# A fourth pair of weight chunks joins the split products of samples 4 to 6

## The chip, the cores and the metric

The kernel runs on 1 core of one Trainium2 chip. The metric is the device time of one execution in microseconds (us); lower is better.

## The reference, cut to what matters

There are eight samples of 256 tokens, each with 1024 features. For each sample a weight matrix (1024x1024) is picked by an index and applied; a quantised feed-forward block follows and is added to the input. A second block (a shared matrix with a low-rank addition, then a mixing of four streams with 50 Sinkhorn rounds) follows.

```
x = x + ffn0(einsum('bij,bkj->bik', x, weight[ids]))     # ffn0: layernorm, int8-quantised w1, gelu, quantised w3
y = x @ base.T + bias + scale * low_rank(x)
x = x + stream_mixing(y)                                 # softmaxes, Sinkhorn, W_branch
```

Only the first product, `x` by `weight[ids]`, is touched by the change. Its result is kept in float32 precision.

## The kernel before, in words

There is no scheduler: each engine's program is written out by hand, and engines meet only at semaphores. A wait holds back everything behind it on its engine. The first block is worked in steps `s` (`step_a`, one on each engine). In step `s` TensorE makes the indexed product of sample `s`, and between its parts the quantised products of samples `s-1` (w1) and `s-2` (w3). The 1024 inputs of the indexed product are worked in four pairs of 128-row chunks (`pr` 0 to 3), and `l0(s, pr)` on TensorE is one such pair, for two token tiles and two halves of 512 outputs.

A pair is worked in one of two ways. Plain (line 1010): 8 matmuls on float32 operands, which the profile shows as 16 records. Parted (line 998): ScalarE copies the pair's `x` and `w` rounded to float32r as high parts (`pair_high`, lines 726 to 732), VectorE subtracts them from the raw values in place to get low parts (`pair_low`, lines 1543 to 1547), and TensorE makes high x high, high x low and low x high: 24 matmuls. Before the change samples 3 to 6 take pairs 0, 1 and 2 parted and pair 3 plain; samples 0 to 2 and 7 are plain throughout.

The orders around it, as written by hand:

- TensorE in step `s` (lines 1140 to 1166): transposes and w3 product of `s-2` between `l0(s,0)` and `l0(s,1)`; transposes of `s-1`, tile 0; `l0(s,2)`; w1 product of `s-1`, tile 0; transposes of tile 1; `l0(s,3)`; w1 product of `s-1`, tile 1. Step 4 ends with `composites_1` (line 1121), which multiplies eight 512 KB chunks of the base weight, loaded into `stage[0]` to `stage[7]`, by the head weights. The first matmul of `l0(s,0)` waits until ScalarE has emptied the accumulators of sample `s-1` (`evac_l0`, line 633).
- ScalarE in step `s` (lines 756 to 806): first quantisation of `s-1` tile 0; `pair_high(s,2)`; evacuations (line 672); `pair_high(s+1,0)` and `(s+1,1)`; quantisation of tile 1 (line 652); evacuation; gelu (line 657) and second quantisation (line 661) of `s-1` tile 0; `evac_l0(s)`; and so on. In steps 6 and 7 it also makes the high parts of the base weight (`split_hi`, line 616): `split_hi(1)` stands behind the second quantisation of sample 5 tile 0, `split_hi(2)` ahead of gelu, root and second quantisation of sample 5 tile 1.
- VectorE in step `s` (lines 1549 to 1573): normalisation of `s-1` tile 0; `finish_w3(s-2,0)`; `pair_low(s,2)`; `layer_norm(s-1,1)`; `finish_w3(s-2,1)`; `pair_low(s+1,0)`, `(s+1,1)`; `finish_w1(s-1,0)` (lines 1461, 1465, 1471 to 1476); `scale_w1(s-1,1)` and so on.
- GpSimd makes the low parts of the base weight (`split_lo`, line 571), each when its high part is there, and adds a bias row to the residual (line 577).
- SyncE issues nearly all DMAs in one order. `load_w(s,pr)` is 1 MB of weights and 256 KB of `x`, and for sample 7 waits until GpSimd has made `split_lo(pr)`. In step 6 its order ends with `load_w(7,1)`, `load_base(3)`, `store_head_rows`, `load_w(7,2)`, `load_w(7,3)`. `store_head_rows` (lines 356 to 359) writes two small arrays, `heads_in` and `bias_in`, to DRAM and counts on `all_st`, which reaches 64 when both have landed.

Buffers overlap by hand as well. `w_hi[3]` lies on `stage[6]` and `stage[7]`, and on `heads_in` and `bias_in`; `w_hi[2]` lies on `stage[4]` and `stage[5]`. Hence this wait, ahead of the last high part:

```
                if pr == PAIRS - 1:
                    act.wait_ge(all_st, 64)
                nc.scalar.activation(w_hi[pr][:, :, :], w_raw[pr][:, :, :], ACT.Copy).then_inc(whi_done, 1)
```

Of the kernel before, what the change touches and what calls it, by code (L numbers as in the profile page):

```python
# [25 lines left out]
def adaln_ffn(nc, x_tok, x_tr, cond_w, ids_cond, ids_lora, gamma, beta, w1, b1, w3, b3, base_w, base_w_nat,  # L26
# [15 lines left out]
    HG = GROUP // 2  # L42
    MIX = 4
    GUEST = NB - 1
    FIRST = 3
    HEADS_1, HEADS_2, HEADS_3 = 4, 5, 6
    TQ = P // NS
    SEL_BANK = 4
# [16 lines left out]
    with ExitStack() as ctx:  # L65
# [14 lines left out]
        one_hi = sb_in(part_e, "one_hi", [1, D], F32R)  # L80
        part_e.close()
        part_n = ctx.enter_context(ExitStack())
        for i in range(2 * PAIRS - 2):
            sb_in(part_n, f"below_heads{i}", [P, D], F32)
        heads_in = sb_in(part_n, "heads_in", [NB * RANK, NH], F32)
        heads_hi = sb_in(part_n, "heads_hi", [NB * RANK, NH], F32R)
# [26 lines left out]

        def parted(s, pr):

            return FIRST <= s < GUEST and pr < PAIRS - 1

        def w_high(pr):

            return w_lo[pr]  # L120

        def x_high(s, pr):

# [1 line left out]

        def parts(s, pr):

            return 2 * (s - FIRST + 1)

        def pair_loads(s, pr):  # L130

# [99 lines left out]


        vec_ld, bias_ld, ids_ld, ones_set = sem("vec_ld"), sem("bias_ld"), sem("ids_ld"), sem("ones_set")
        high = [sem(f"high{i}") for i in range(PAIRS - 1)]
        low = [sem(f"low{i}") for i in range(PAIRS - 1)]
        id_zero, id_set, id16_set = sem("id_zero"), sem("id_set"), sem("id16_set")
        misc_ld, wb_split, b_set, b_ld = sem("misc_ld"), sem("wb_split"), sem("b_set"), sem("b_ld")
        st_ld = [sem(f"st_ld{i}") for i in range(ST)]
# [5 lines left out]
        wld = [sem(f"wld{i}") for i in range(PAIRS)]  # L244
        first_ld = sem("first_ld")
        whi_done, wlo_done, l0_pair, l0_evac = sem("whi_done"), sem("wlo_done"), sem("l0_pair"), sem("l0_evac")
        ln_mean, ln_var = sem("ln_mean"), sem("ln_var")
        ln_step, ln_sqrt, q1_done, q2_done = sem("ln_step"), sem("ln_sqrt"), sem("q1_done"), sem("q2_done")
        t1_done, e1_done, m1_done, o1_done = sem("t1_done"), sem("e1_done"), sem("m1_done"), sem("o1_done")
        t3_done, e3_done, m3_done, o3_done = sem("t3_done"), sem("e3_done"), sem("m3_done"), sem("o3_done")  # L250
# [47 lines left out]
        def _(sp):  # L298
# [100 lines left out]
            load_w(2, 3)  # L399

            def step_a(s):
                nat = KC if s == HEADS_1 else 0
                load_w(s + 1, 0)
                for c in range(0, nat, 2):
                    load_nat(c)
                load_w(s + 1, 1)
                store_x1(s - 2, 0)
                for c in range(1, nat, 2):
                    load_nat(c)
                load_w(s + 1, 2)  # L410
                store_x1(s - 2, 1)
                load_w(s + 1, 3)
                load_xres(s - 1)

            def step_a_base(s):
                load_base(0)
                store_x1(s - 2, 0)
                load_base(1)
                load_w(s + 1, 0)
                store_x1(s - 2, 1)  # L420
                load_base(2)
                load_xres(s - 1)
                load_w(s + 1, 1)
                load_base(3)
                store_head_rows()
                load_w(s + 1, 2)
                load_w(s + 1, 3)

# [181 lines left out]
        def _(act):  # L610
            def split_hi(pr):

                act.wait_ge(wld[pr], pair_loads(GUEST - 1, pr) + 16)
                if pr == PAIRS - 1:
                    act.wait_ge(all_st, 64)
                nc.scalar.activation(w_hi[pr][:, :, :], w_raw[pr][:, :, :], ACT.Copy).then_inc(whi_done, 1)

# [18 lines left out]
            def statistics(s, t):  # L636
                j = NTOK * s + t
                act.wait_ge(l0_evac, j + 1)
                nc.scalar.activation(lnst[:, t, 0:1], lnst[:, t, 1:2], ACT.Copy, scale=-1.0 / D).then_inc(ln_mean, 1)
                act.wait_ge(ln_mean, j + 1)  # L640
                wait(act, x1_st[t], 16 * (s - 1))
                nc.scalar.activation(ln_sq(s, t)[:, :], hbuf[t][:, :], ACT.Square, bias=lnst[:, t, 0:1],
                                     accum_out=lnst[:, t, 10:11]).then_inc(ln_var, 1)

            def ln_root(s, t):
                j = NTOK * s + t
# [79 lines left out]
            def pair_high(s, pr):  # L726
                if s < NB and parted(s, pr):
                    act.wait_ge(wld[pr], pair_loads(s, pr))
                    if s == FIRST:
                        act.wait_ge(all_st, 32)  # L730
                    nc.scalar.activation(x_high(s, pr), x_raw[pr][:, :, :], ACT.Copy).then_inc(high[pr], 1)
                    nc.scalar.activation(w_high(pr)[:, :, :], w_raw[pr][:, :, :], ACT.Copy).then_inc(high[pr], 1)
# [23 lines left out]
            def step_a(s):  # L756
                quant1(s - 1, 0)
                if s == 2:
                    rows_high()
                pair_high(s, 2)  # L760
                if s == HEADS_2:
                    composites_2()
                evac_T(s - 2, 1, 3)
                if s == GUEST:
                    split_hi(3)
                ln_root(s - 1, 1)
                evac_T(s - 1, 0, 1)
                pair_high(s + 1, 0)
# [36 lines left out]
                quant2(s - 1, 1)  # L805
                statistics(s, 1)
# [583 lines left out]
        def _(dve):  # L1390
# [26 lines left out]
            def centre(s, t):  # L1417

                h = hbuf[t]
                dve.wait_ge(ln_var, NTOK * s + t + 1)  # L1420
# [128 lines left out]
            def step_a(s):  # L1549
                normalise(s - 1, 0)  # L1550
                if s == 2:
                    rows_low()
                    dve.wait_ge(sc_ev, 2)
                if s == FIRST:
                    gate_first()
                if s == HEADS_2:
                    composites()
# [1 line left out]
                pair_low(s, 2)  # L1559
                layer_norm(s - 1, 1)  # L1560
                finish_w3(s - 2, 1)
                pair_low(s + 1, 0)
                pair_low(s + 1, 1)
                finish_w1(s - 1, 0)
# [342 lines left out]
```

## Time and profile before

| what | us |
|---|---|
| median of 3 runs (749.0 to 750.52) | 749.83 |
| the profiled execution, its own time | 751.13 |
| span of the profiled execution, first to last instruction | 749.3 |
| TensorE busy in it | 707.8 (94%) |
| VectorE busy | 526.2 (70%) |
| ScalarE busy | 397.3 (53%) |
| GpSimd busy | 79.9 (11%) |

The profile is of one execution. All times in rows are microseconds from the start of its span. The granted clock of TensorE had a mean of 0.977 of full speed. Steps 4, 5 and 6 of the first block fill the stretch from 166 to 305 us. A busy TensorE isn't TensorE at its peak, because matmuls overlap and their ends are modelled; the chain of work is the better measure of what one block of matmuls costs.

### The profile page before, as it was taken

The numbers are of one execution on the slowest core, as the hardware profiler recorded it, in microseconds if no ns is written. First come the engines' busy times: TensorE is split into PE (matmuls) and PEld (weight loads), VectorE is DVE, ScalarE is ACT, GpSimd is POOL, SyncE is SP. The second block draws the span as 40 slices with busy tenths as digits, with TensorE's granted clock in tenths as the row PEclk, the third lists the DMA queues.
The fourth block names the chain that finished last, engine by engine and source line by source line (L and its number), as shares of the span: only waits on it lengthen the run. The fifth ranks groups of instructions, "written<-read, shape, count | busy, mean of one in ns | idle before, by whom it ended". The sixth has DMA issues, their size and how long they took to land.

```text
span 749.3 us, 10394 instructions
## 1 busy us (share of the span) xinstructions
PE 707.8 (94%) x3292; PEld 477.6 (64%) x3292; DVE 526.2 (70%) x1869; ACT 397.3 (53%) x714; POOL 79.9 (11%) x57
## 2 busy tenths in 40 slices
PE   8999999999999999999998999999999993999957
PEld 5444445656536565445656888887888872677656
DVE  4569676979742976776663341428899998999985
ACT  1255846666741584828355443444534432899614
POOL 0201400302030032732040000000000000000000
PEclk9999999999999999999998999999999996999979
DMA  7997255558734236851232303303123086847106
GB/s 297 409 410 284 94 196 207 187 165 300 294 111 169 101 126 197 327 199 64 69 127 74 127 13 115 127 0 128 56 74 128 0 281 224 262 162 244 64 1 224
DMA packets 52477, 124.35 MB, mean 166 GB/s; under 512 B 6211, under 2 KB 31939, under 8 KB 46920
## 3 DMA queue, kind: packets, MB, share of 16 engines
q1 hardware_dynamic: 51128, 120.96, 45.6%
q10 hardware_dynamic: 1296, 2.74, 1.0%
q8 instruction: 26, 0.43, 0.2%
q14 instruction: 27, 0.22, 0.1%
HBM read 97.96 MB, written 25.72 MB: 165 GB/s over the span
## 4 chain that ended last, share of the span: by engine, by line
PE 74%; DVE 19%; ACT 5%; issue 2%; DMA 1%; SPq 0%; ACTq 0%; DVEq 0%
PE PS L1204 20%; PE PS L1010 18%; PE PS L1087 13%; PE PS L998 8%; DVE kprod L1725 4%; DVE ksum L1729 4%; PE PS L1192 2%; PE PS L1019 2%; DVE ka L1732 2%; DVE kb L1732 2%; PE PS L1356 2%; PE PS L1121 2%; PE PS L1178 2%; PE PS L1238 1%; PE PS L1366 1%
## 5 line engine op out<-in xcount | busy, mean ns | idle before, releaser
L1010 PE MATMUL PS<-w_raw,x_raw 128*128 128x512 f32 x320 | 141.7, 596 | 1.3 <-DMA w_raw<-cond_w_dram 0.9
L1010 PEld LDWEIGHTS PS<-w_raw,x_raw 128*128 128x128 f32 x320 | 59.4, 190 | 69.6 <-issue 69.6
L1204 PE MATMUL PS<-w_hi,xT_hi 128*128 128x512 f32 x256 | 103.0, 402 | 0.0
L1204 PE MATMUL PS<-w_hi,xT_lo 128*128 128x512 f32 x256 | 100.5, 393 | 0.0
L1204 PE MATMUL PS<-w_lo,xT_hi 128*128 128x512 f32 x256 | 100.4, 392 | 0.0
L1539 DVE TENSOR_TENSOR xT_lo<-PS,xT_hi 128x512 fp32r<-128x512 f32 x32 | 20.5, 682 | 66.0 <-ACT xT_hi L753 66.0
L1729 DVE TENSOR_REDUCE ksum<-kprod 128x16 f32<-128x64 f32 x392 | 66.3, 211 | 0.0
L577 POOL TENSOR_TENSOR xres<-xres,vecs 128x1024 f32<-128x1024 f32 x16 | 42.5, 2680 | 218.1 <-DMA xres<-x_tok_dram 218.1
L672 ACT ACTIVATE qT<-PS,round_c 128x1024 bf16<-128x1024 f16 x32 | 35.4, 1108 | 56.6 <-PE PS L1019 56.6
L1087 PE MATMUL PS<-w3q,qT 128*128 128x512 bf16 x256 | 57.8, 379 | 1.0 <-ACT qT L672 1.0
L1087 PE MATMUL PS<-w1q,qT 128*128 128x512 bf16 x256 | 57.9, 379 | 0.3 <-ACT qT L672 0.3
L1204 PEld LDWEIGHTS PS<-w_hi,xT_lo 128*128 128x128 f32 x256 | 48.3, 189 | 10.4
L1204 PEld LDWEIGHTS PS<-w_lo,xT_hi 128*128 128x128 f32 x256 | 48.5, 190 | 9.2
L1204 PEld LDWEIGHTS PS<-w_hi,xT_hi 128*128 128x128 f32 x256 | 48.6, 190 | 9.1
L833 ACT ACTIVATE y<-PS 128x512 f32<-128x512 f32 x32 | 18.0, 592 | 57.0 <-PE PS L1212 57.0
L1087 PEld LDWEIGHTS PS<-w1q,qT 128*128 128x128 bf16 x256 | 24.5, 98 | 32.6 <-issue 5.5
L1087 PEld LDWEIGHTS PS<-w3q,qT 128*128 128x128 bf16 x256 | 24.2, 98 | 33.2 <-issue 4.4
L1461 DVE SCALAR_TENSOR_TENSOR gbuf<-PS,lnst,vecs 128x512 f32<-128x512 f32 x32 | 23.5, 748 | 30.9 <-PE PS L1087 30.8
L998 PE MATMUL PS<-w_lo 128*128 128x512 f32 x96 | 38.6, 402 | 1.2 <-DVE w_low L1547 1.0
L998 PE MATMUL PS<-w_lo,x_low 128*128 128x512 f32 x96 | 38.0, 395 | 0.0
L998 PE MATMUL PS<-w_low,w_lo 128*128 128x512 f32 x96 | 37.8, 394 | 0.0
L1488 DVE SCALAR_TENSOR_TENSOR x1buf<-PS,q2st,vecs 128x512 f32<-128x512 f32 x32 | 23.0, 746 | 19.1 <-PE PS L1087 19.1
(209 smaller groups left out, 1358.0 us busy)
## 6 DMA issues: line engine op xcount, KB each, us to landing
w_raw<-cond_w_dram SPq DMA_DIRECT2D x31, 1024.0 KB, 5.4
x_raw<-x_tr_dram SPq DMA_DIRECT2D x32, 256.0 KB, 6.7
stage<-w_dram SPq DMA_DIRECT2D x16, 512.0 KB, 16.2
xres<-x_tok_dram SPq DMA_DIRECT2D x8, 1024.0 KB, 8.2
x_scratch<-x1buf SPq DMA_DIRECT2D x16, 512.0 KB, 6.7
x1n<-x_scratch SPq DMA_DIRECT2D x16, 512.0 KB, 6.6
y_scratch<-y SPq DMA_DIRECT2D x16, 512.0 KB, 3.7
stage<-base_w_nat_dram SPq DMA_DIRECT2D x8, 512.0 KB, 8.7
```

Source lines behind the costliest of these rows:

```text
L577: nc.gpsimd.tensor_tensor(xres[:, t, :], xres[:, t, :], vecs[:, V_B3, :], ALU.add).then_inc(xb3_done, 1)
L672: nc.scalar.activation(qT[t][:, :, :], PS[:, T_BANK + t, :].bitcast(F16).rearrange("p (c n) -> p c n", c=KC), ACT.Identity, bias=round_c[: ...
L998: mm = pe.matmul(PS[:, 2 * t + h, :], xx[:, c, t * P:(t + 1) * P], ws[:, c, h * H2:(h + 1) * H2], start=(pr == 0 and c == 0 and xx is xh a ...
L1010: mm = pe.matmul(PS[:, 2 * t + h, :], x_raw[pr][:, c, t * P:(t + 1) * P], w_raw[pr][:, c, h * H2:(h + 1) * H2], start=(pr == 0 and c == 0) ...
L1087: mm = pe.matmul(PS[:, O_BANK + h, :], qT[t][:, c, :], wq[:, c, h * H2:(h + 1) * H2], start=(c == 0), stop=(c == KC - 1))
L1204: pe.matmul(PS[:, 2 * t + h, :], xx[:, c, t * P:(t + 1) * P], ws[c // 2][:, c % 2, h * H2:(h + 1) * H2], start=(c == 0 and xx is xT_hi and ...
L1461: nc.vector.scalar_tensor_tensor(out=g[:, h * H2:(h + 1) * H2], in0=PS[:, O_BANK + h, :], scalar=lnst[:, t, 8:9], in1=vecs[:, V_SW1, h * H ...
L1488: nc.vector.scalar_tensor_tensor(out=x1buf[t][:, h * H2:(h + 1) * H2], in0=PS[:, O_BANK + h, :], scalar=q2st[:, t, 1:2], in1=vecs[:, V_SW3 ...
L1539: nc.vector.tensor_tensor(xT_lo[:, 4 * h:4 * h + 4, t * P:(t + 1) * P], PS[:, T_BANK + h, :].rearrange("p (c n) -> p c n", c=4), xT_hi[:, ...
L1725: nc.vector.tensor_tensor(kprod[i][:, :, :, :], (kmat if row else kmat_t)[i][:, :, :, :], cols(v, HG), ALU.mult).then_inc(k_step[i], 1)
L1729: nc.vector.tensor_reduce(ksum[i][:, :, :], kprod[i][:, :, :, :], AX.X, ALU.add).then_inc(k_step[i], 1)
L1732: nc.vector.reciprocal(new[i][:, :, :], ksum[i][:, :, :]).then_inc(k_step[i], 1)
```

## The change

Pair 3 of samples 4, 5 and 6 becomes parted. Its high `w` goes into `w_hi[3]`, its high `x` into the last quarter of `w_lo[3]`. `pair_high(s,3)` is put on ScalarE behind the evacuation of tile 0, `pair_low(s,3)` on VectorE behind `finish_w3(s-2,1)`, in both cases ahead of the parts of the next sample. Since `w_hi[3]` is now in use during step 4, chunks 6 and 7 of the base weight are loaded at the end of that step, behind `load_w(5,3)`. Since it is in use until step 6, `heads_in` and `bias_in` move down by two buffers, onto `w_hi[2]`; so `split_hi(2)` and no longer `split_hi(3)` waits for `all_st`, and `store_head_rows` is issued ahead of `load_base(3)`. Two semaphores of the statistics become one with doubled counts.

```
-    FIRST = 3
+    FIRST = (3, 3, 3, 4)
...
-        for i in range(2 * PAIRS - 2):
+        for i in range(2 * PAIRS - 4):
             sb_in(part_n, f"below_heads{i}", [P, D], F32)
...
-            return FIRST <= s < GUEST and pr < PAIRS - 1
+            return FIRST[pr] <= s < GUEST
...
-            return w_lo[pr]
+            return w_hi[pr] if pr == PAIRS - 1 else w_lo[pr]
...
-            return 2 * (s - FIRST + 1)
+            return 2 * (s - FIRST[pr] + 1)
...
-        high = [sem(f"high{i}") for i in range(PAIRS - 1)]
-        low = [sem(f"low{i}") for i in range(PAIRS - 1)]
+        high = [sem(f"high{i}") for i in range(PAIRS)]
+        low = [sem(f"low{i}") for i in range(PAIRS)]
...
-        ln_mean, ln_var = sem("ln_mean"), sem("ln_var")
+        ln_stat = sem("ln_stat")
...
             def step_a(s):
-                nat = KC if s == HEADS_1 else 0
+                nat = KC - 2 if s == HEADS_1 else 0
...
                 load_w(s + 1, 3)
+                for c in range(nat, KC if nat else 0):
+                    load_nat(c)
                 load_xres(s - 1)
...
                 load_w(s + 1, 1)
+                store_head_rows()
                 load_base(3)
-                store_head_rows()
...
-                if pr == PAIRS - 1:
+                if pr == PAIRS - 2:
                     act.wait_ge(all_st, 64)
...
                     split_hi(3)
                 ln_root(s - 1, 1)
                 evac_T(s - 1, 0, 1)
+                if s < GUEST:
+                    pair_high(s, 3)
                 pair_high(s + 1, 0)
                 pair_high(s + 1, 1)
                 quant1(s - 1, 1)
...
                 layer_norm(s - 1, 1)
                 finish_w3(s - 2, 1)
+                if s < GUEST:
+                    pair_low(s, 3)
                 pair_low(s + 1, 0)
                 pair_low(s + 1, 1)
                 finish_w1(s - 1, 0)
```

## Rows read from the trace of the kernel before

**Rows 1.** The page: TensorE's busy time, and GB/s moved in 40 slices.

```profile
PE 707.8 (94%) x3292; PEld 477.6 (64%) x3292; DVE 526.2 (70%) x1869; ACT 397.3 (53%) x714; POOL 79.9 (11%) x57
...
GB/s 297 409 410 284 94 196 207 187 165 300 294 111 169 101 126 197 327 199 64 69 127 74 127 13 115 127 0 128 56 74 128 0 281 224 262 162 244 64 1 224
```

**Rows 2.** The chain that ended last, step 4: start, duration, what.

```profile
186.00 5.62 PE PS L998 x24
...
195.53 6.92 PE PS L1010 x16
...
205.91 0.89 issue
206.80 13.89 PE PS L1121 x32
```

**Rows 3.** Timeline of VectorE, step 4: start, duration, line, operation, tiles, idle time before.

```profile
193.39 0.68 DVE L1546 TENSOR_TENSOR x_low<-x_raw,w_lo 128x512 fp32r<-128x512 f32 x1
...
196.19 1.40 DVE L1461 SCALAR_TENSOR_TENSOR gbuf<-PS,lnst,vecs 128x512 f32<-128x512 f32 x2
...
205.95 0.75 DVE L1461 SCALAR_TENSOR_TENSOR gbuf<-PS,lnst,vecs 128x512 f32<-128x512 f32 x1 [0.91 <-PE PS L1087]
```

**Rows 4.** The DMA issues of the page: count, KB each, us to landing.

```profile
stage<-base_w_nat_dram SPq DMA_DIRECT2D x8, 512.0 KB, 8.7
```

**Rows 5.** The chain that ended last, end of step 5.

```profile
255.17 2.20 DVE w_low L1547
257.37 1.33 DVE gbuf L1461 x2
...
263.86 1.10 ACT hbuf L633 x2
...
265.10 5.82 PE PS L998 x24
```

**Rows 6.** Timeline of ScalarE, steps 4, 6 and 7.

```profile
187.11 0.62 ACT L731 ACTIVATE w_lo<-x_raw 128x512 fp32r<-128x512 f32 x1
...
189.44 0.61 ACT L731 ACTIVATE w_lo<-x_raw 128x512 fp32r<-128x512 f32 x1
...
299.12 1.24 ACT L661 ACTIVATE gbuf<-gbuf,round_c,q2st 128x1024 f32<-128x1024 f32 x1 [1.67 <-DVE q2st L1476]
...
307.17 1.90 ACT L616 ACTIVATE w_hi<-w_raw 128x2048 fp32r<-128x2048 f32 x1
...
311.69 1.24 ACT L661 ACTIVATE gbuf<-gbuf,round_c,q2st 128x1024 f32<-128x1024 f32 x1 [0.16 <-DVE q2st L1476]
```

**Rows 7.** Timeline of GpSimd, step 6.

```profile
290.14 4.52 POOL L571 TENSOR_TENSOR w_lo<-w_raw,w_hi 128x2048 fp32r<-128x2048 f32 x1 [14.12 <-ACT w_hi L616]
302.24 4.54 POOL L571 TENSOR_TENSOR w_lo<-w_raw,w_hi 128x2048 fp32r<-128x2048 f32 x1 [7.58 <-ACT w_hi L616]
```

**Rows 8.** Timeline of VectorE, step 6.

```profile
294.25 1.50 DVE L1465 TENSOR_TENSOR gbuf<-gbuf,vecs 128x1024 f32<-128x1024 f32 x1
...
305.07 2.78 DVE L1465 TENSOR_TENSOR gbuf<-gbuf,vecs 128x1024 f32<-128x1024 f32 x1
```

**Rows 9.** Timeline of SyncE's DMA queue, steps 5 to 7.

```profile
261.16 0.35 SPq L320 DMA_DIRECT2D w_raw<-cond_w_dram  x1
...
270.44 0.24 SPq L350 DMA_DIRECT2D bias_in<-biashead_scratch  x1
...
306.96 0.35 SPq L320 DMA_DIRECT2D w_raw<-cond_w_dram  x1
...
309.11 0.43 SPq L358 DMA_DIRECT2D stack_low_scratch<-heads_in  x1
```

**Rows 10.** Timeline of TensorE, step 7.

```profile
314.90 0.61 PE L1019 MATMUL PS<-ident,gbuf 128*128 128x128 f16 x8
```

**Rows 11.** Timeline of TensorE, later: a pause.

```profile
403.05 1.19 PE L1212 MATMUL PS<-es,ls 128*128 128x512 f32 x4 [1.56 <-DVE ls L1581]
```

**Rows 12.** Busy time by stretch: length, each engine's busy time (instructions), granted clock, DMA.

```profile
404.00:412.00 8.00, 6.90 (x31) 5.89 (x30) 2.76 (x6) 7.69 (x17) 0.46 (x1) 0.57 0.03 9
```

More of the change, by code:

```diff
@@ L44, in adaln_ffn @@
     GUEST = NB - 1
-    FIRST = 3
+    FIRST = (3, 3, 3, 4)
     HEADS_1, HEADS_2, HEADS_3 = 4, 5, 6
@@ L82, in adaln_ffn @@
         part_n = ctx.enter_context(ExitStack())
-        for i in range(2 * PAIRS - 2):
+        for i in range(2 * PAIRS - 4):
             sb_in(part_n, f"below_heads{i}", [P, D], F32)
@@ L114, in parted @@
         def parted(s, pr):
-            return FIRST <= s < GUEST and pr < PAIRS - 1
+            return FIRST[pr] <= s < GUEST
         def w_high(pr):
-            return w_lo[pr]
+            return w_hi[pr] if pr == PAIRS - 1 else w_lo[pr]
         def x_high(s, pr):
@@ L126, in parts @@
         def parts(s, pr):
-            return 2 * (s - FIRST + 1)
+            return 2 * (s - FIRST[pr] + 1)
         def pair_loads(s, pr):
@@ L233, in adaln_ffn @@
         vec_ld, bias_ld, ids_ld, ones_set = sem("vec_ld"), sem("bias_ld"), sem("ids_ld"), sem("ones_set")
-        high = [sem(f"high{i}") for i in range(PAIRS - 1)]
-        low = [sem(f"low{i}") for i in range(PAIRS - 1)]
+        high = [sem(f"high{i}") for i in range(PAIRS)]
+        low = [sem(f"low{i}") for i in range(PAIRS)]
         id_zero, id_set, id16_set = sem("id_zero"), sem("id_set"), sem("id16_set")
@@ L246, in adaln_ffn @@
         whi_done, wlo_done, l0_pair, l0_evac = sem("whi_done"), sem("wlo_done"), sem("l0_pair"), sem("l0_evac")
-        ln_mean, ln_var = sem("ln_mean"), sem("ln_var")
+        ln_stat = sem("ln_stat")
         ln_step, ln_sqrt, q1_done, q2_done = sem("ln_step"), sem("ln_sqrt"), sem("q1_done"), sem("q2_done")
@@ L401, in step_a @@
             def step_a(s):
-                nat = KC if s == HEADS_1 else 0
+                nat = KC - 2 if s == HEADS_1 else 0
                 load_w(s + 1, 0)
@@ L412, in step_a @@
                 load_w(s + 1, 3)
+                for c in range(nat, KC if nat else 0):
+                    load_nat(c)
                 load_xres(s - 1)
@@ L423, in step_a_base @@
                 load_w(s + 1, 1)
+                store_head_rows()
                 load_base(3)
-                store_head_rows()
                 load_w(s + 1, 2)
@@ L613, in split_hi @@
                 act.wait_ge(wld[pr], pair_loads(GUEST - 1, pr) + 16)
-                if pr == PAIRS - 1:
+                if pr == PAIRS - 2:
                     act.wait_ge(all_st, 64)
@@ L638, in statistics @@
                 act.wait_ge(l0_evac, j + 1)
-                nc.scalar.activation(lnst[:, t, 0:1], lnst[:, t, 1:2], ACT.Copy, scale=-1.0 / D).then_inc(ln_mean, 1)
-                act.wait_ge(ln_mean, j + 1)
+                nc.scalar.activation(lnst[:, t, 0:1], lnst[:, t, 1:2], ACT.Copy, scale=-1.0 / D).then_inc(ln_stat, 1)
+                act.wait_ge(ln_stat, 2 * j + 1)
                 wait(act, x1_st[t], 16 * (s - 1))
                 nc.scalar.activation(ln_sq(s, t)[:, :], hbuf[t][:, :], ACT.Square, bias=lnst[:, t, 0:1],
-                                     accum_out=lnst[:, t, 10:11]).then_inc(ln_var, 1)
+                                     accum_out=lnst[:, t, 10:11]).then_inc(ln_stat, 1)
             def ln_root(s, t):
@@ L728, in pair_high @@
                     act.wait_ge(wld[pr], pair_loads(s, pr))
-                    if s == FIRST:
+                    if s == FIRST[0]:
                         act.wait_ge(all_st, 32)
@@ L767, in step_a @@
                 evac_T(s - 1, 0, 1)
+                if s < GUEST:
+                    pair_high(s, 3)
                 pair_high(s + 1, 0)
@@ L1419, in centre @@
                 h = hbuf[t]
-                dve.wait_ge(ln_var, NTOK * s + t + 1)
+                dve.wait_ge(ln_stat, 2 * (NTOK * s + t + 1))
                 nc.vector.tensor_scalar(lnst[:, t, 2:3], lnst[:, t, 10:11], 1.0 / D, LN_EPS, ALU.mult, ALU.add).then_inc(ln_step, 1)
@@ L1553, in step_a @@
                     dve.wait_ge(sc_ev, 2)
-                if s == FIRST:
+                if s == FIRST[0]:
                     gate_first()
@@ L1561, in step_a @@
                 finish_w3(s - 2, 1)
+                if s < GUEST:
+                    pair_low(s, 3)
                 pair_low(s + 1, 0)
```

## The prediction

> **What bounds the kernel now.** I read the page first: TensorE is busy 94% of the span [rows 1], so a shorter product on TensorE should shorten the kernel, unless another engine is what ends the waits there. Then the chain that ended last, in order of time. In step 4 it is TensorE all the way, with 0.89 us of pause ahead of `composites_1` [rows 2]. A parted pair takes 5.62 us of it and the plain one 6.92 us: 1.30 us for each of three pairs, 3.9 us in all, is what the edit offers.
>
> At the end of step 5 the chain isn't TensorE's. It goes through VectorE's `w_low` for pair 1 of the next sample, then without a pause into `gbuf` (L1461, the start of `finish_w1(4,0)`), through gelu and second quantisation into the evacuation `evac_l0(5)` at 263.86, and only then into `l0(6,0)` at 265.10 [rows 5]. Whatever is put on VectorE ahead of `finish_w1` there is paid in full.
>
> **Step 4.** The low parts of a pair cost VectorE 2.80 us (start to start, 193.39 to 196.19) [rows 3], the high parts cost ScalarE 2.33 us (187.11 to 189.44) [rows 6]. `finish_w1(3,0)` moves from 196.19 to 199.0. Its way to the start of the second quantisation is 5.35 us, by the same way in step 5 (257.37 to 263.86, less 1.15 for the quantisation) [rows 5, 6], so VectorE is free at 204.4 and has the two halves of `scale_w1(3,1)` done 1.4 us later, at 205.8. `composites_1` waits for exactly that; before it came 0.1 us behind the second half, which ended at 206.70 [rows 2, 3]. So it starts at 205.9: the gain of step 4 is 0.9 and not 1.3 us. ScalarE's extra 2.33 us delays the quantisation of tile 1 by as much, to about 195.3, some 0.2 us behind where TensorE asks for it; this is inside the 0.4 lost.
>
> Chunks 6 and 7 are now issued behind `load_w(5,3)`, near 202.4. A chunk takes 8.7 us to land [rows 4]; chunk 6 is wanted at three quarters of the 13.89 us of `composites_1` [rows 2], at 216.3, chunk 7 at 218. I cost this at nothing; the residual load behind them gets later by the 2.6 us that 1 MB takes at 410 GB/s, the page's best early slice [rows 1], and nothing asks for it soon. If that cover were gone the price would be some us, ahead of step 5.
>
> **Step 5.** Everything starts 0.9 us early, VectorE then gets 2.80 us more ahead of `finish_w1(4,0)`: +1.9. `evac_l0(5)` ends and `l0(6,0)` starts at 267.0 and not at 265.1. TensorE has meanwhile saved its 1.3 us, and waits.
>
> **Step 6.** `l0(6,3)` saves 1.3 us on TensorE, but the other engines get busier. ScalarE has 2.33 us more ahead of `split_hi(0)`, so GpSimd can begin its first split some 2.8 us later than 290.14 [rows 7]. What that does is in two rows: `gbuf` (L1465) at 294.25 took 1.50 us and ended 1.09 us behind the end of GpSimd's split (290.14 + 4.52); at 305.07 it took 2.78 us and ended 1.07 us behind the next (302.24 + 4.54) [rows 7, 8]. That VectorE operation stands still until GpSimd is done. With GpSimd's split ending at 297.4 to 298.8, the add of `finish_w1(5,0)` ends at 298.5 to 299.9 instead of 295.75, and the second quantisation of sample 5 tile 0, at 299.12 before [rows 6], is later by 2.1 to 3.5 us. I take 3.0. Behind it on ScalarE stands `split_hi(1)`, behind that GpSimd's `split_lo(1)`, and for that SyncE waits before `load_w(7,1)`: from 306.96 [rows 9] to 310.0.
>
> **Step 7, the moved wait.** `split_hi(2)` ran at 307.17 with nothing to wait for [rows 6]. Now it waits for `all_st`, and the two stores that raise it are issued on SyncE only behind `load_w(7,1)`. Moving them ahead of `load_base(3)` helps little: before they were issued at 309.11, 2.15 us behind `load_w(7,1)` with `load_base(3)` between [rows 9]; now some 1.7 us behind it. All of them are queued behind 1.25 MB. The trace has no row for their landing, but a near one: two small stores behind `load_w(6,3)`, with 1 MB of residual between, were waited for until 270.44, 9.3 us after that load was issued at 261.16 [rows 9]. Less 2.6 us for the 1 MB leaves 6.7 us. Bounds: 1.9 us after the load is issued (they land at once) and 9.3 us. I take 6.7, the same queue with the same load ahead: `split_hi(2)` starts at 316.7 (bounds 311.9 and 319.3).
>
> The Trainium skill speaks against the change here (DMA: Bandwidth & Descriptors, section Queues, rings and completion order): an engine's count on the semaphore lands only after every earlier write of that DMA engine. By it the small stores count no sooner than the 1.25 MB ahead has landed, and the lower bound falls away; that agrees with the 9.3 us of the row.
>
> Queued behind `split_hi(2)` on ScalarE are gelu, root and second quantisation of sample 5 tile 1. That quantisation starts 4.52 us behind `split_hi(2)` (307.17 to 311.69) and takes 1.15 [rows 6]; TensorE's transposes of it, between `product(5,0,3)` and `l0(7,1)`, follow at 316.7 + 5.8 = 322.5. They ran at 315.0 [rows 10], when TensorE was just ready for them. **So TensorE's work restarts 7.5 us late** (bounds 317.7 and 325.1: +2.7 and +10.1), and nearly all of it is a pause: it would have been ready by 317. GpSimd's splits and the loads for pairs 2 and 3 of sample 7 follow `split_hi(2)` too, but TensorE has two pairs of 7 us each and two products before it asks for the last.
>
> **The clock.** A pause of 5 to 6 us hasn't been free in this trace. After one of 1.56 us at 403.05 and 1.1 us more [rows 11] the granted clock fell, and had a mean of 0.57 over the eight us from 404, that is, mostly at the lower level of 1.2 GHz [rows 12]. That cost at most 0.43 x 8 = 3.4 us, less where TensorE paused anyway. I take 2.5 (bounds 0 and 3.4).
>
> **The sum.** The step 4 and 5 terms (-0.9, +2.8), the step 6 term (+1.1 on the way through ScalarE and GpSimd) and the wait for the stores are all within the +7.5; +2.5 for the clock makes +10.0. From 410 us on the order of work is the same and TensorE-bound or Sinkhorn-bound, so nothing is won back. Against the profiled execution's 751.13 that gives 761.1; it lies 1.3 above the median of the runs, so in their terms 749.83 + 10.0 = **759.8 us**. The folded semaphore of the statistics adds and removes no instruction and no wait that ends later: nothing.
>
> **The rivals.**
> 1. The pause comes as told but is short, or the clock stays up: the stores land early or GpSimd doesn't get in VectorE's way. +2.7 to +7, 752.5 to 757. For it: no row times these stores. Against: the 9.3 us of the neighbour.
> 2. The stores are harmless, and only VectorE's queue in step 5 costs. Then `l0(7,0)` starts when `evac_l0(6)` is done: `split_hi(1)` ahead of it is 3.0 late, so some +1.5: 751.3. It decides if `all_st` is up by 310. Against: SyncE doesn't even issue the stores until then.
> 3. All is hidden and TensorE alone counts: 3 x 1.3 = -3.9, 745.9. It would need `finish_w1(4,0)` to have slack in step 5; the chain shows none [rows 5]. If the copies took less time on VectorE than the 2.80 of their twins, it would come nearer.
> 4. Both pauses (the one ahead of `l0(6,0)` is some 3 us in two pieces) drop the clock and the stores take the full 9.3: +10.1 + 3.4 = +13.5, 763.3, or somewhat more.
> That the parted pair 3 isn't faster than the plain one is hardly open: the shapes are those of pairs 0 to 2.
>
> **Chances.** Forecast with a drop in the clock, 757 to 763.3: 0.62. Rival 1: 0.20. Rival 2: 0.08. Rival 3: 0.04. Rival 4 and beyond: 0.06. About 0.2% (1.5 us) is what a measurement of this kernel can tell from no change. Faster by more 0.05, within 0.08, slower 0.87. The range, 753.0 to 763.5, holds the forecast and rival 1.
>
> **What would show it.** Right: L998 x24 at 5.6 us for pair 3; `composites_1` about 0.9 us earlier; `l0(6,0)` near 267; two small stores issued near 312; an idle time of ScalarE of 6 to 9 us ahead of the `split_hi` of pair 2, ended by a DMA; TensorE idle ahead of L1019 near 317, 4 to 7 us; a granted clock under 1 near 322 to 328. Wrong: `split_hi(2)` with no idle time before it, or `l0(6,0)` at 265 or earlier.

## The result and the profile after

| | median us (lowest to highest, runs) | against the kernel before, 95% interval |
|---|---|---|
| before | 750.17 (749.0 to 751.2, 4) | |
| after | 762.97 (761.02 to 764.68, 4) | 1.0173 [1.0154, 1.0193] |

The change makes the kernel 12.8 us slower. The forecast was 759.8 us with a range of 753.0 to 763.5: the sign and the place were right, the median lies 3.2 us above the forecast and inside the range. The profiled execution took 761.02 us (span 759.1); it is the fastest of the four, and stands 9.9 us above the profiled execution of before, where +10.0 was forecast.

The page's totals. TensorE is busy for less time than before [rows 1], in a span 9.8 us longer: the shorter product is there, and it doesn't decide.

```profile
PE 705.0 (93%) x3316; PEld 480.1 (63%) x3316; DVE 537.8 (71%) x1875; ACT 404.2 (53%) x720; POOL 80.1 (11%) x57
```

The chain that ended last, from step 4 to step 7 (start, duration, what):

```profile
195.48 5.61 PE PS L1002 x24
...
205.46 13.89 PE PS L1125 x32
...
256.62 2.21 DVE w_low L1551
258.83 1.33 DVE gbuf L1465 x2
...
266.56 7.35 PE PS L1002 x24
...
292.95 3.48 PE PS L1091 x16
...
297.24 2.65 DVE gbuf L1469
...
303.80 1.90 ACT w_hi L618
305.77 4.54 POOL w_lo L573
...
311.82 6.32 DMA stack_low_scratch<-bias_in
318.23 1.91 ACT w_hi L618
...
324.05 1.03 PE PS L1023 x8
325.08 8.87 PE PS L1014 x16
...
337.85 6.92 PE PS L1014 x16
```

Pair 3 now takes 5.61 us (first line) instead of 6.92 [rows 2]. `composites_1` starts at 205.46 instead of 206.80. From step 5 on the kernel is late: `l0(6,0)` starts at 266.56 instead of 265.10 [rows 5] and then takes 7.35 us instead of 5.82. Near 300 the chain has left TensorE altogether and runs through VectorE, ScalarE, GpSimd and two small stores to TensorE's restart at 324.05. Before, the same transposes started at 314.90 [rows 10]. In the order of time (us from the start of the span):

| event | before | after | forecast |
|---|---|---|---|
| `composites_1` starts | 206.80 | 205.46 | 205.9 |
| `l0(6,0)` starts | 265.10 | 266.56 | 267.0 |
| second quantisation, sample 5 tile 0 | 299.12 | 302.65 | 302.1 |
| `load_w(7,1)` issued | 306.96 | 310.48 | 310.0 |
| `split_hi(2)` starts | 307.17 | 318.23 | 316.7 |
| TensorE's transposes behind it start | 314.90 | 324.05 | 322.5 |

The end of the chain's detour, on SyncE's queue:

```profile
310.48 0.35 SPq L320 DMA_DIRECT2D w_raw<-cond_w_dram  x1
...
311.35 0.43 SPq L358 DMA_DIRECT2D stack_low_scratch<-heads_in  x1
311.82 0.42 SPq L359 DMA_DIRECT2D stack_low_scratch<-bias_in  x1
```

and on ScalarE:

```profile
302.65 1.24 ACT L663 ACTIVATE gbuf<-gbuf,round_c,q2st 128x1024 f32<-128x1024 f32 x1 [1.68 <-DVE q2st L1480]
...
318.23 1.91 ACT L618 ACTIVATE w_hi<-w_raw 128x2048 fp32r<-128x2048 f32 x1 [8.16 <-DMA stack_low_scratch<-bias_in]
```

Here ScalarE stood for 8.16 us at the moved wait, with gelu and the second quantisation of tile 1 queued behind it. The last of the small stores had landed 7.7 us after `load_w(7,1)` was issued.

TensorE's own timeline shows the two pauses:

```profile
265.47 0.62 PE L1023 MATMUL PS<-ident,gbuf 128*128 128x128 f16 x8 [2.22 <-ACT gbuf L663]
...
324.05 1.03 PE L1023 MATMUL PS<-ident,gbuf 128*128 128x128 f16 x8 [6.66 <-ACT gbuf L663]
```

and the windows by stretch (length, busy time of PE, PEld, DVE, ACT, POOL, granted clock, DMA share, GB/s) show what stands behind each:

```profile
268.00:272.00 4.00, 4.00 (x13) 3.12 (x12) 2.17 (x2) 3.95 (x6) 3.33 (x2) 0.64 0.01 1
...
324.00:328.00 4.00, 3.95 (x12) 2.29 (x13) 3.90 (x5) 1.84 (x4) 4.00 (x3) 0.50 0.51 172
...
416.00:424.00 8.00, 6.37 (x38) 5.31 (x38) 3.21 (x8) 7.69 (x16) 0.45 (x1) 1.00 0.02 5
```

Behind both pauses TensorE works at the lower level for a while (a mean of 0.64, and then 0.50, which is 1.2 GHz). That costs 1.5 us in `l0(6,0)` (7.35 against 5.82) and 1.9 us in `l0(7,1)` (8.87; the same product takes 6.92 at 337.85), with 0.4 us more in the transposes ahead of the latter (1.03 against 0.61 [rows 10]). In the last window the clock is at its full 2.4 GHz, although a pause of 1.56 us ended shortly ahead of it, at 414.52, as long as the one behind which the execution profiled before had a fall [rows 11, 12]. This is part of why the two profiled executions are only 9.9 us apart, and the medians 12.8.

### The profile page after: what moved, and what is told of

The parts are those of the page before. It is cut to its first block, busy times and chain, and to the rows that moved or that the text cites. A ratio compares the mean times of both kernels' runs of the same rounds, so it can differ in the third digit from the quotient of the medians.

```text
span 759.1 us, 10454 instructions
## 1 busy us (share of the span) xinstructions
PE 705.0 (93%) x3316; PEld 480.1 (63%) x3316; DVE 537.8 (71%) x1875; ACT 404.2 (53%) x720; POOL 80.1 (11%) x57
## 4 chain that ended last, share of the span: by engine, by line
PE 66%; DVE 20%; ACT 7%; issue 2%; DMA 2%; SPq 1%; POOL 1%; ACTq 0%; DVEq 0%
PE PS L1208 18%; PE PS L1014 14%; PE PS L1091 11%; PE PS L1002 8%; DVE kprod L1731 4%; DVE ksum L1735 4%; PE PS L1023 2%; DVE ka L1738 2%; DVE kb L1738 2%; PE PS L1196 2%; PE PS L1360 2%; PE PS L1125 2%; PE PS L1242 1%; PE PS L1182 1%; DMA x_raw<-x_tr_dram 1%
## 5 line engine op out<-in xcount | busy, mean ns | idle before, releaser
L1014 PE MATMUL PS<-w_raw,x_raw 128*128 128x512 f32 x272 | 122.4, 604 | 1.6 <-ACT hbuf L635 0.8
L1014 PEld LDWEIGHTS PS<-w_raw,x_raw 128*128 128x128 f32 x272 | 51.3, 193 | 61.4 <-issue 61.0
L1002 PE MATMUL PS<-w_low,w_lo 128*128 128x512 f32 x120 | 48.0, 400 | 0.0
```

The costliest lines, as they stand in the source:

```text
L1002: mm = pe.matmul(PS[:, 2 * t + h, :], xx[:, c, t * P:(t + 1) * P], ws[:, c, h * H2:(h + 1) * H2], start=(pr == 0 and c == 0 and xx is xh a ...
L1014: mm = pe.matmul(PS[:, 2 * t + h, :], x_raw[pr][:, c, t * P:(t + 1) * P], w_raw[pr][:, c, h * H2:(h + 1) * H2], start=(pr == 0 and c == 0) ...
```

## The experiments

Each difference in us below is the kernel's median less the median of the kernel before in the same set of runs; that one was 750.53 for e1 to e4, 749.52 for e5 to e8, and 750.15 for e9 to e11. The change stands at +12.8 by the same measure. The ratio and its interval are computed apart from the medians and can differ from them by up to a tenth of a per cent.

**e1: the stores on another queue.** The parted pairs stay; `store_head_rows` is now a function of ScalarE that waits for `all_low` to reach 4 and issues the same two stores.

```
                 load_w(s + 1, 1)
-                store_head_rows()
                 load_base(3)
...
                 quant2(s - 1, 0)
                 if s == GUEST - 1:
+                    store_head_rows()
                     split_hi(1)
```

> The changed kernel, with the two small stores issued from ScalarE's own DMA queue ahead of split_hi(1) and no longer from SyncE behind load_w(7,1). Theory (the wait for the stores costs most of the time): the stores are issued near 304 and land before ScalarE gets to split_hi(2) near 310, which then has no idle time before it; TensorE's pause of 6.7 us near 317 and the low clock behind it go away. Only the lateness of l0(7,0), 1.9 us, stays: 752 us, ratio to before 1.002 to 1.004. Rival (the stores are harmless, the extra copies on VectorE and ScalarE cost the time): stays above 758 us, ratio above 1.010.

Measured: 754.38 us (750.28 to 756.34, 10 runs), 1.0052 [1.0035, 1.0069]. On ScalarE:

```profile
303.71 0.62 ACTq L615 DMA_DIRECT2D stack_low_scratch<-bias_in  x1
...
311.31 1.91 ACT L622 ACTIVATE w_hi<-w_raw 128x2048 fp32r<-128x2048 f32 x1 [0.64 <-DMA stack_low_scratch<-bias_in]
```

The wait has shrunk from 8.16 to 0.64 us, and of the +12.8 us only +3.85 are left. So the wait for the stores is the main cost: 12.8 - 3.85 = 9.0 us. What is left is some 2 us more than I had expected here; 1.5 of them are the lower clock behind the first pause, which I had counted as free. In e1's chain `l0(6,0)` is slow too: it starts at 267.30 and takes 7.35 us.

**e2: the stores one place earlier on SyncE.**

```
+                store_head_rows()
                 load_w(s + 1, 1)
-                store_head_rows()
                 load_base(3)
```

> The changed kernel, with store_head_rows still on SyncE but one place earlier, ahead of load_w(7,1). It is then issued when VectorE has the low parts, near 303, and not when GpSimd has split_lo(1), near 310; ahead of it in the queue are the loads issued from 299 to 301.4 (3.75 MB). Theory: those take about 9 us at 410 GB/s, so the stores land near 311 to 313, split_hi(2) waits 1 to 3 us instead of 8.2, its quantisation ends near 317 to 319, TensorE pauses at most 1 us; no low clock: 752 to 754 us. Rival (the landing is slow by itself, whatever is ahead): waits as long after the issue as before, lands near 310 or sooner, no idle time, as with the stores on ScalarE's queue: 752 us.

Measured: 757.28 us (754.9 to 757.63, 4), 1.0087 [1.0063, 1.0111], +6.75: a miss, over 3 us above what was expected. The chain of e2:

```profile
303.80 10.25 DMA stack_low_scratch<-bias_in
...
320.58 8.62 PE PS L1014 x16
```

The stores were issued 8 us earlier than after the change, but landed only 10.25 us later, behind big loads issued from 299.5 to 301.6. In e1 they were issued at the same time from ScalarE's queue and had landed by 311.3, 2.8 us sooner than here. So moving an instruction in a queue moved its issue by 8 us and its landing by only 4. The pause on TensorE was now 2.0 us long, and yet `l0(7,1)` took 8.62 us. A short pause cost nearly as much clock as the long one.

**e4: the moved wait alone, on the kernel before.** No pair is added; the small arrays lie on `w_hi[2]`, as the change has them.

```
-        for i in range(2 * PAIRS - 2):
+        for i in range(2 * PAIRS - 4):
...
                 load_w(s + 1, 1)
+                store_head_rows()
                 load_base(3)
-                store_head_rows()
...
-                if pr == PAIRS - 1:
+                if pr == PAIRS - 2:
                     act.wait_ge(all_st, 64)
```

> The kernel before, with only the moved buffers of heads_in and bias_in, the wait for all_st at split_hi(2), and the stores ahead of load_base(3): no pair 3 is parted. Theory: load_w(7,1) at 307.0, the stores land 7.7 us behind it as in the changed kernel, at 314.7, TensorE restarts at 320.5 (+5.4), and the clock falls for some 4 us (+1.9): +7 to +8, 757 to 758 us, ratio 1.009 to 1.011. Rival (the wait costs only together with the late steps 5 and 6): +3 or less, ratio under 1.004.

Measured: 756.43 us (754.24 to 758.24, 4), 1.0084 [1.0055, 1.0113], +5.9. Its rows: SyncE,

```profile
306.58 0.35 SPq L320 DMA_DIRECT2D w_raw<-cond_w_dram  x1
```

ScalarE,

```profile
314.58 1.91 ACT L616 ACTIVATE w_hi<-w_raw 128x2048 fp32r<-128x2048 f32 x1 [7.69 <-DMA stack_low_scratch<-bias_in]
```

and TensorE.

```profile
320.40 1.03 PE L1019 MATMUL PS<-ident,gbuf 128*128 128x128 f16 x8 [5.72 <-ACT gbuf L661]
```

`split_hi(2)` comes 8.0 us behind the load, as after the change (7.75). The wait needs none of the new pairs to hurt. After the change TensorE restarts 3.65 us later than here, and `load_w(7,1)` is 3.9 us later: the lateness that steps 5 and 6 collect is added in full ahead of the wait. e1 and e4 each take one of the two causes out, and their +3.85 and +5.9 add up to 9.8 and not to 12.8 us: together the causes cost some 3 us more than apart, and no run shows where.

**e3: pair 3 of sample 5 left plain.** Samples 4 and 6 stay parted; the wait stays moved.

```
-            return FIRST[pr] <= s < GUEST
+            return s in (4, 6) if pr == PAIRS - 1 else FIRST[pr] <= s < GUEST
```

> The changed kernel, with pair 3 parted for samples 4 and 6 only and plain for 5. Theory: VectorE's queue in step 5 is back to what it was, l0(6,0) starts at 263.8 to 264.3 instead of 266.6 without a low clock behind it; step 6 is late on GpSimd by 1 to 2 us only, load_w(7,1) is issued near 307, the stores land near 314.7, TensorE restarts near 320.4 with a low clock: +5.4 + 1.9 = +7 to +8 to before, 757 to 758 us, some 5 less than the changed kernel. Rival (step 5 costs nothing because the pause in step 7 would swallow it): same as the changed kernel.

Measured: 759.36 us (758.2 to 761.95, 4), 1.012 [1.01, 1.014], +8.8: 4.0 us below the change, and 1.4 above the upper end of what was expected. `l0(6,0)` starts at 266.46 and not near 264, though it waits for nothing new: in this execution the clock had fallen at 228 to 236 us (last section). Without the copies in step 5 the wait is still there, 7.74 us of it:

```profile
317.17 1.91 ACT L618 ACTIVATE w_hi<-w_raw 128x2048 fp32r<-128x2048 f32 x1 [7.74 <-DMA stack_low_scratch<-bias_in]
```

**e5: e1 and e3 together.** No new lines.

> Pair 3 parted for samples 4 and 6 only, and the two stores from ScalarE's queue. Theory: both priced causes are gone, the wait for the stores and VectorE's longer queue in step 5; what is left is the gain of step 4 (1.3 us) against the lateness in step 6 by GpSimd's split standing in VectorE's way (its add of 3.6 us instead of 1.5 in the run with the stores on SyncE): within 1.5 us of the kernel before, 749 to 751.5 us. Rival (the 3.9 us that are left with the stores alone moved come from step 6 or the extra copies there, not from step 5): stays at 753 to 754.5.

Measured: 750.33 us (748.82 to 752.43, 10), 1.0012 [1.0, 1.0024], +0.8. Both losses out, and the kernel is level with the one before. Its chain has `l0(6,0)` at 264.65 and at its normal length:

```profile
206.35 13.89 PE PS L1130 x32
...
264.65 5.78 PE PS L1007 x24
```

So sample 5's pair is worth e1 less e5, 3.85 - 0.81 = +3.0 us. In the traces its TensorE gain is more than lost by the 2.80 us on VectorE's path, as the prediction had it, and by the clock behind the pause that this makes.

In this profile `composites_1` starts at 206.35 and not at 205.46, although the program up to there is that of after the change. 0.6 us of this come from 30 us earlier: GpSimd's addition of the bias row to the residual started at 171.95 here and at 173.23 after the change, and so met another operation of VectorE (the first line is e5, the second after the change):

```profile
172.80 2.60 DVE L1449 SCALAR_TENSOR_TENSOR hbuf<-hbuf,lnst,vecs 128x1024 f32<-128x1024 f32 x1
```

```profile
177.04 2.68 DVE L1497 TENSOR_TENSOR x1buf<-x1buf,xres 128x1024 f32<-128x1024 f32 x1
```

Each takes some 1.25 us in the profiles where GpSimd meets the other one. The profiles of e1 to e5 have the first form, those of both kernels and of e7 to e11 the second; where pair 3 of sample 4 is parted, the first form costs step 4 0.6 us (e1, e2, e3, e5 against after, e7, e9 to e11). What decides between them isn't shown.

**e6: keep sample 5, change VectorE's order.** On e1; `pair_low(s+1,1)` steps back behind `finish_w1(s-1,0)` and `scale_w1(s-1,1)`, so that the path of step 5 is clear.

```
                 pair_low(s + 1, 0)
-                pair_low(s + 1, 1)
                 finish_w1(s - 1, 0)
...
                     scale_w1(s - 1, 1)
+                    pair_low(s + 1, 1)
                     centre(s, 0)
```

> All of the change, the two stores from ScalarE's queue, and on VectorE pair_low(s+1,1) behind scale_w1(s-1,1), where VectorE waited for ScalarE's statistics, and not ahead of finish_w1(s-1,0). Theory: finish_w1(4,0) starts 2.8 us earlier, near 256, l0(6,0) starts at 263.8 to 264.5 with no pause of TensorE of over 1 us ahead of it and no low clock behind it; step 6 stays late by 1 to 2 us. 749 to 751.5 us, at least 3 less than with the stores alone moved. Rival (the order on VectorE doesn't matter, the sum of its work does): 753.5 to 755, as with the stores alone moved.

Measured: 757.85 us (754.16 to 762.38, 6), 1.0112 [1.008, 1.0143], +8.3: worse than e1 by 4.5 us, a miss. In its new place the copy delays the normalisation at the start of the next step. ScalarE, step 4:

```profile
183.68 1.25 ACT L658 ACTIVATE hbuf<-hbuf,round_c,lnst 128x1024 f32<-128x1024 f32 x1 [3.15 <-DVE lnst L1457]
```

and the chain:

```profile
214.02 13.89 PE PS L1130 x32
```

`composites_1` is 7 us behind the kernel before. Nearly all of the loss is there, in steps 3 and 4. In step 5 the new order did what was expected of it: `l0(6,0)` starts at 272.32, 58.30 us behind `composites_1`, exactly as in the kernel before (61.10 after the change), and takes 5.79 us, with no low clock. So of the two places tried, the old one is on TensorE's path in step 5 and the new one in steps 3 and 4. The new order in step 5 alone wasn't tried.

**e7 and e8: one sample at a time.** Both on e1, with the set of samples for pair 3 as `(4,)` in e7 and `(6,)` in e8.

> Pair 3 parted for sample 4 only, the two stores from ScalarE's queue. Theory: composites_1 starts 1.3 us earlier as in the changed kernel, steps 5 and 6 are as before; the stores are issued near 301 and land near 308.5, so split_hi(2), wanted near 305.8, waits some 2.7 us, of which TensorE sees 0.5 to 1.5. 748.5 to 750.5 us. Rival (nothing of step 4's gain arrives): 750.5 to 752.

> Pair 3 parted for sample 6 only, the two stores from ScalarE's queue. Theory: l0(6,3) takes 5.6 instead of 6.9 us but the second quantisation of sample 5 tile 0 comes 1.5 to 3 us later than in the kernel before, because GpSimd's split_lo(0) starts 2.5 to 4 us later and VectorE's add stands behind it; evac_l0(6) and so l0(7,0) are 1 to 1.5 us later than before: 750 to 752 us. Rival (step 6 gives its 1.3 us): l0(7,0) at 303.5 or earlier, 749.2 or less.

e7: 748.12 us (747.31 to 749.92, 10), 0.9985 [0.9973, 0.9998], -1.4. `composites_1` starts at 205.24 and `split_hi(2)` waits for nothing, where I had expected 2.7 us of waiting (the last store was issued at 298.17, and not near 301):

```profile
305.63 1.89 ACT L622 ACTIVATE w_hi<-w_raw 128x2048 fp32r<-128x2048 f32 x1
```

e8: 751.68 us (749.28 to 753.69, 10), 1.0023 [1.001, 1.0037], +2.2: sample 6 alone costs although its pair is 1.3 us shorter on TensorE. GpSimd and ScalarE in e8:

```profile
292.38 6.07 POOL L572 TENSOR_TENSOR w_lo<-w_raw,w_hi 128x2048 fp32r<-128x2048 f32 x1 [14.74 <-ACT w_hi L622]
```

```profile
299.57 1.06 ACT L663 ACTIVATE gbuf<-gbuf 128x1024 f32<-128x1024 f32 x1 [1.69 <-DVE gbuf L1474]
```

The split took 6.07 us instead of 4.52 [rows 7], and gelu waited 1.69 us for VectorE. `load_w(7,1)` comes later by this detour, and `l0(7,1)` waits for it:

```profile
311.44 6.80 DMA x_raw<-x_tr_dram
```

It starts at 318.29 and in the kernel before at 315.51. This profile also has a fall of the clock at 228 to 236 us, in step 5, where nothing was changed; by it `l0(6,0)` is already 1.5 us late (266.60 against 265.10). So the detour is worth 1.3 us here, on top of the 1.3 us that the pair saves. The runs say the same with less precision: those of e8 whose mean granted clock was 0.984 took 749.28 to 750.54 us (3 of 10), the other seven 751.63 to 753.69, and the kernel before at 0.984 had a median of 749.2 in this set. At an equal clock sample 6's pair costs some 0.7 us; whether it also makes the falls more frequent isn't shown.

**e9: sample 4 alone, nothing moved.** The stores, the wait and the small arrays are as before the change, and only pair 3 of sample 4 is parted.

```
-            return FIRST[pr] <= s < GUEST
+            return s in (4,) if pr == PAIRS - 1 else FIRST[pr] <= s < GUEST
```

> Pair 3 parted for sample 4 only, with heads_in and bias_in, the wait at split_hi(3) and the order of SyncE as in the kernel before; only chunks 6 and 7 of the base weight are loaded at the end of step 4. Theory: step 4 gives 1.3 us and nothing takes it back: 748.0 to 749.0 us, ratio 0.9975 to 0.9990, and never slower than the run with the stores on ScalarE's queue. Rival (the 1.3 us are lost again in step 5, where VectorE is late anyway): ratio 0.9995 to 1.0005.

Measured: 748.62 us (747.8 to 750.96, 11), 0.9986 [0.9976, 0.9997], -1.5. This version is 1.5 us below the kernel before by the medians and 0.14% by the ratio; the interval only just leaves out 1, and the difference is no more than the 1.5 us that the prediction took for the least one can tell. With e7 it shows that sample 4's pair needs neither the moved arrays nor the stores' new place.

**e10: `split_hi(2)` behind the second quantisation of tile 1.** All three pairs and the moved wait stay; what was queued behind the wait now stands ahead.

```
-                if s == GUEST - 1:
-                    split_hi(2)
                 gelu(s - 1, 1)
                 ln_root(s, 0)
                 quant2(s - 1, 1)
+                if s == GUEST - 1:
+                    split_hi(2)
```

> The changed kernel with split_hi(2), and so its wait for the stores, behind the second quantisation of sample 5 tile 1 on ScalarE and not ahead of gelu. Theory (what costs is the work queued behind the wait): the stores still land near 318, but the quantisation ends near 316 and TensorE's transposes at 317 have no pause; GpSimd's split_lo(2) still ends near 324.7 and load_w(7,2) lands near 331, where l0(7,2) wants it near 328.5: a pause of 2 to 3 us moves there and the low clock is rarer. 757 to 759.5 us, 3.5 to 6 less than the changed kernel. Rival (the wait itself costs, wherever it stands): 762 to 764 us.

Measured: 759.47 us (758.04 to 760.38, 4), 1.0128 [1.0111, 1.0145], +9.3: 3.5 below the change. TensorE:

```profile
318.66 0.61 PE L1023 MATMUL PS<-ident,gbuf 128*128 128x128 f16 x8
...
331.17 7.13 PE L1014 MATMUL PS<-w_raw,x_raw 128*128 128x512 f32 x16 [1.08 <-DMA x_raw<-x_tr_dram]
...
341.33 3.79 PE L1091 MATMUL PS<-w1q,qT 128*128 128x512 bf16 x10 [3.03 <-DVE x1buf L1492]
```

The long pause at the transposes is gone, and 4.1 us of pauses stand later instead: the loads and VectorE's evacuations that follow `split_hi(2)` are late next. Less than half of the 9 us came back, because the wait also holds up the splits and loads themselves.

**e11: the stores behind `load_base(3)`**, in the order of before, to price the one part of the move that was meant to help.

```
-                store_head_rows()
                 load_base(3)
+                store_head_rows()
```

> The changed kernel with store_head_rows behind load_base(3), as in the kernel before. Theory: 1 MB more lies ahead of the stores in the same queue; they land 2 to 3 us later, near 320.5, and TensorE restarts as much later: 765 to 766.5 us, 2 to 3.5 more than the changed kernel. Rival (small stores are not held up by what is ahead of them in the queue): 762 to 764 us, landing near 318.5.

Measured: 764.86 us (764.27 to 765.17, 4), 1.0203 [1.0187, 1.0219], +14.7: 1.9 above the change. `split_hi(2)` starts 2.7 us later:

```profile
311.62 0.35 SPq L320 DMA_DIRECT2D w_raw<-cond_w_dram  x1
```

```profile
313.62 7.21 DMA stack_low_scratch<-bias_in
320.92 1.91 ACT w_hi L618
```

Of these 2.7 us 1.1 aren't the order's: `load_w(7,1)` is issued at 311.62 and not at 310.48, behind a split of GpSimd of 5.38 instead of 4.54 us. From that issue to the stores' landing it is 9.2 us here and 7.7 after the change, so 1 MB more ahead of them is worth 1.5 us. The reorder saved at most 1.9 us of a wait that cost nine.

## Why the prediction was right, and where it was off

**The sum of the parts.** Adding to sample 4 alone (e7) first sample 6 (e5), then sample 5 (e1), then the stores' old place on SyncE (the change):

| part | from | us |
|---|---|---|
| sample 4's pair | e7 | -1.4 |
| sample 6's pair | e5 less e7 | +2.2 |
| sample 5's pair | e1 less e5 | +3.0 |
| the wait for the stores | the change less e1 | +9.0 |
| sum | | +12.8 |

The sum comes out by construction, but two parts have a second reading: e8 alone gives sample 6 +2.2 again, and e3 less e5 gives the stores 8.8 - 0.8 = +8.0. The sizes are rougher than the digits. In the profiles of e5 and e7, 1.1 of the 1.9 us between them stand at `composites_1` already, ahead of anything that belongs to sample 6 (0.6 of them by the form in which GpSimd met VectorE); e8's +2.2 has falls of the clock in it. What the traces give to sample 6's pair itself is 0.6 (e5) to 1.3 us (e8). The last part isn't the wait alone (e4: +5.9): it holds what the two causes cost more together than apart.

**Step 4, -0.9.** The trace of after is already 0.5 us early ahead of step 4 (TensorE's transposes there start at 184.88 instead of 185.39), so of the 1.34 us at `composites_1` 0.84 belong to the step. The traces of e7 and e9 give 0.85 by the same reckoning. Right, for this form of the meeting of GpSimd and VectorE; in e1 and e5, with the other, the step gained 0.2.

**Step 5, +1.9.** `l0(6,0)` is 1.46 us late, 1.96 counted from that head start. Right, and e5 shows that taking the copies away takes it away. The step had no term for the clock behind this pause (2.22 us idle, then 0.62 of transposes, then 0.47): **1.5 us put at nothing.** It stood in rival 4 alone.

**Step 6, +3.0: about the right number, for the wrong reason.** The quantisation came 3.5 us late, at the upper bound of 3.5. The prediction made this of 1.9 us from step 5 and 1.1 from GpSimd's split. But VectorE's add started 3.0 us late (297.24 against 294.25 [rows 8]) before GpSimd had held it at all, because TensorE's product ahead of it was that late (292.95 in the chain above). In the trace of before:

```profile
289.95 3.47 PE PS L1087 x16
```

These 3.0 us are the 1.46 of step 5 and the 1.53 of its lower clock. What GpSimd's hold on the add then cost ScalarE is the rest of the 3.5, half a microsecond:

```profile
299.91 1.06 ACT L659 ACTIVATE gbuf<-gbuf 128x1024 f32<-128x1024 f32 x1 [0.54 <-DVE gbuf L1469]
```

So a term that was 0.6 too large stood in for one of 1.5 that was missing; that the sum came near was luck. The hold itself is real. The rows of VectorE after the change, beside those of GpSimd:

```profile
297.24 2.64 DVE L1469 TENSOR_TENSOR gbuf<-gbuf,vecs 128x1024 f32<-128x1024 f32 x1
...
306.78 4.60 DVE L1469 TENSOR_TENSOR gbuf<-gbuf,vecs 128x1024 f32<-128x1024 f32 x1
```

```profile
293.88 4.92 POOL L573 TENSOR_TENSOR w_lo<-w_raw,w_hi 128x2048 fp32r<-128x2048 f32 x1 [19.50 <-ACT w_hi L618]
...
305.77 4.53 POOL L573 TENSOR_TENSOR w_lo<-w_raw,w_hi 128x2048 fp32r<-128x2048 f32 x1 [6.96 <-ACT w_hi L618]
```

The splits end at 298.80 and 310.30, the adds at 299.88 and 311.38: each 1.08 us behind, however early it began. The same add beside no split took 1.22 us (e8, at 305.27, begun just ahead of one). The Trainium skill (SBUF — State Buffer, section SBUF: two separate sides) states that the port pair which VectorE and GpSimd share is locked for a whole instruction, and that a VectorE operation with two SBUF inputs meets GpSimd's reads there. The trace agrees in both directions: 4.60 us for the add above, and e8's 6.07 us for a split that was due at 292.38 while VectorE's copy ran until 294.0; from there it is the usual 4.5 us to its end at 298.45.

**Step 7, the stores' landing: 6.7 us taken, 7.7 measured** (7.9 in e4), inside the bounds of 1.9 and 9.3. With the 0.5 us of a later load this puts `split_hi(2)` at 318.2 instead of 316.7 and TensorE's restart at +9.1 instead of +7.5. The mechanism was right and the term 1 us too small: I had taken the 1 MB of the neighbouring row off the 9.3 us at the page's best rate, 2.6 us. e11 has that row's order and its 9.2 us, and shows that the 1 MB is worth 1.5; 9.3 less 1.5 would have given 7.8. The rule of the Trainium skill that the prediction cites (DMA: Bandwidth & Descriptors, Queues, rings and completion order) agrees with this as far as it can be seen: where TensorE waited for `load_w(7,1)` itself, the load had landed 6.5 to 7.2 us behind its issue (e5, e6, e8), and the stores behind it never came before 7.7. No trace shows both landings.

**The clock, 2.5.** Behind the long pause 2.3 us were measured (1.9 in `l0(7,1)`, 0.4 in the transposes): right. The row that this was taken from was misread a little: of the two pauses named, the one of 1.1 us came behind the start of the fall, at 407.40 and not ahead of it.

**Why the sum still came near.** In the profiled execution +10.0 was forecast and +9.9 measured. `l0(7,1)` ends 11.4 us later than before: 9.1 at the transposes and 2.3 for the clock. Then 2.0 us come back, because the fall of the clock at 404 to 412 in the execution profiled before [rows 12] has no twin in the one profiled after, and some 0.4 are lost again. So the forecast was 1.4 us too small up to there and met the number by a difference between two executions: luck. In the medians the change costs 12.8. Of the 2.9 us that the profiled executions don't show, 1.0 is that the one profiled before was slower than its median, and 1.9 that the one profiled after was the fastest of four. **The terms that were mis-sized are the stores' landing (6.7 for 7.7 us) and the clock behind the first pause (nothing for 1.5 us)**; the rest of the 3.2 us in the medians stays open. The four runs after the change lie in two pairs, 761.02 and 761.71, 764.22 and 764.68. One more fall of the clock would suit the gap, but their mean granted clocks (0.977 and 0.977, 0.978 and 0.975) don't bear it out.

**The rivals.** Rival 1 (the clock stays up): no, 0.50 behind the pause. Rival 2 (stores harmless): e1 brings its case about. It came out at 754.4 and not 751.3; 1.5 us of this are the clock behind the first pause, the rest isn't shared out. Rival 3 (all hidden, -3.9): only sample 4's pair showed a gain, 1.4 and 1.5 us by the medians of e7 and e9, 1.1 by their ratios and 0.85 in their traces, against 1.3 us saved on TensorE. Rival 4 (both pauses drop the clock, the stores take 9.3): both did, with 7.7 for the stores; its +13.5 is nearest to the medians, but by a longer wait than there was.

## What to carry to other kernels

An edit that shortens the busiest engine's work is worth only what stands there when that engine is the last to be waited for: of three equal savings of 1.3 us one came through, and two lost more by the copies that pay for them on VectorE and ScalarE. When a buffer moves, follow the semaphore that frees it: a wait moved one place earlier held up the whole queue of ScalarE behind two tiny stores that had themselves to wait for a megabyte of loads. Price a pause of TensorE by its length and by the slower product behind it.

## What the runs showed of the hardware that I hadn't expected

The granted clock fell behind short pauses in some executions and not in others. The pause ahead of `l0(6,0)`, 2.22 us idle, 0.62 of transposes and some 0.5 idle, stands alike in five profiles. In four of them (after, e1, e2, e10) the clock fell and the product took 6.84 to 7.37 us; in e11 it didn't:

```profile
267.02 5.79 PE PS L1002 x24
```

The same holds for the 1.56 us ahead of the matmuls of line 1212: a fall before [rows 11, 12], none after the change. In e2 it fell behind a pause of 2.0 us ahead of `l0(7,1)` (8.62 instead of 6.92). In e3 it fell with no pause at all, behind the very small matmuls of step 5 (24 columns) and the transposes that follow them (the windows of e3, columns as above):

```profile
224.00:228.00 4.00, 4.00 (x27) 3.51 (x25) 0.00 (x0) 1.98 (x2) 0.00 (x0) 1.00 0.13 25
228.00:232.00 4.00, 4.00 (x42) 3.44 (x42) 0.36 (x1) 1.69 (x4) 0.00 (x0) 0.77 0.82 307
232.00:236.00 4.00, 4.00 (x16) 3.18 (x15) 0.00 (x0) 0.00 (x0) 0.00 (x0) 0.81 0.00 1
```

TensorE is busy for all of 224 to 236, and the clock still has a mean of 0.77 and 0.81 there. The same order of work ran through this stretch at full clock in the profile after the change, and fell in those of e8 and e10. So such a fall comes in some executions and not in others. Behind the pauses it was worth 1.0 to 2.6 us in the product that followed (5.82 to 6.84 us in e2, 6.92 to 9.51 in e3), as much as the effects of e5, e7 and e8, and their runs scatter by 2.6 to 4.4 us.

On ScalarE's own queue the small store was still some 7.5 us on its way (303.71 to 311.3 in e1; 7.3 in e5, e6 and e8), against 10.25 us for the same store issued at the same time on SyncE's (e2). So another queue gave it an earlier issue and 2.8 us, and no quick way past the loads that SyncE had issued.
